# A matrix-memory cell's causal mask: from a product per decay tile to the unused rows of the decays' own operands

## The reference, cut to what matters

```
log_f_cum = concatenate([zeros, cumsum(log_sigmoid(fg), axis=2)], axis=2)
log_fg = where(ltr, (log_f_cum - log_f_cum^T)[:, :, 1:, 1:], -inf)
log_D = log_fg + ig^T
max_log_D = max(log_D, axis=-1)
D = exp(log_D - max_log_D)
C = (q @ k^T / sqrt(dh)) * D
Cn = C / (max(|C.sum(-1)|, exp(-max_log_D)) + EPS)
h = Cn @ v          # then normalised over dh and scaled
```

## Time and profile before

| | us |
|---|---|
| median of 3 runs | 823.45 (821.46 to 826.2) |
| the profiled execution, its own time | 822.99 |
| the profiled execution, span of the instructions | 821.2 |
| TensorE busy | 720.1 (88%) |
| VectorE busy | 503.7 (61%) |
| ScalarE busy | 418.2 (51%) |
| GpSimd busy | 387.2 (47%) |

### The profile page before, as it was taken

The page is one execution under the profiler, slowest core; times in us unless marked ns, Lnnn a source line. Parts: engine busy times, 40 slices in busy tenths (PEclk is TensorE's granted clock), DMA queues, the critical chain, the costliest instruction groups (busy, mean ns, idle before and its releaser), DMA issues.

```text
span 821.2 us, 20216 instructions
## 1 busy us (share of the span) xinstructions
PE 720.1 (88%) x7408; PEld 607.1 (74%) x7408; DVE 503.7 (61%) x992; ACT 418.2 (51%) x849; POOL 387.2 (47%) x587
## 2 busy tenths in 40 slices
PE   0874089999999998299999999999999999999993
PEld 0542057677767766178889999899999999999992
DVE  4772726667676766786525979443465767676740
ACT  0765336666666665443436323222456666666651
POOL 3111145778777776332211254214236575757553
PEclk9998559999999999599999999999999999999997
DMA  7882183545353530448772321332468888888854
GB/s 257 275 276 88 45 248 109 145 132 163 117 174 109 171 105 3 156 154 306 247 249 102 103 98 57 93 101 68 160 229 213 259 217 256 218 254 220 253 122 51
DMA packets 90720, 135.57 MB, mean 165 GB/s; under 512 B 16720, under 2 KB 44112, under 8 KB 90672
## 3 DMA queue, kind: packets, MB, share of 16 engines
q1 hardware_dynamic: 74128, 107.41, 39.8%
q0 software_dynamic: 7168, 17.04, 10.4%
q10 hardware_dynamic: 9376, 10.49, 3.9%
HBM read 92.32 MB, written 34.21 MB: 154 GB/s over the span
## 4 chain that ended last, share of the span: by engine, by line
PE 52%; DVE 3%; DMA 2%; POOL 1%; ACT 1%; issue 0%; SPq 0%; POOLq 0%; ACTq 0%
PE psH L1184 31%; PE psY L1201 15%; PE psT L1164 2%; PE psR L1225 2%; DMA xT<-over13l 1%; PE psT L1233 1%; DVE xnorm L1591 1%; DMA out<-ystage,sidx 1%; DVE xl L1414 1%; DVE stats L1482 1%; POOL out L1680 1%; PE psG L1240 1%; DVE over13h L1591 1%; ACT over13l L1362 0%; DVE over2l L1582 0%
## 5 line engine op out<-in xcount | busy, mean ns | idle before, releaser
L1184 PE MATMUL psH<-xh,w13h 128*128 128x256 f32 (+1 forms) x768 | 222.7, 290 | 3.0 <-DVE w13l L1426 3.0
L1184 PE MATMUL psH<-xh,w13l 128*128 128x256 f32 (+1 forms) x768 | 216.6, 282 | 0.0
L1184 PE MATMUL psH<-xl,w13h 128*128 128x256 f32 (+1 forms) x768 | 216.0, 281 | 0.0
L1648 POOL TENSOR_TENSOR hl<-sg,hh 128x256 fp32r<-128x256 f32 (+1 forms) x96 | 78.5, 823 | 212.8 <-ACT hh L1299 212.3
L1184 PEld LDWEIGHTS psH<-xh,w13h 128*128 128x128 f32 (+1 forms) x768 | 138.6, 180 | 12.2 <-issue 7.6
L1184 PEld LDWEIGHTS psH<-xl,w13h 128*128 128x128 f32 (+1 forms) x768 | 138.9, 181 | 0.7
L1184 PEld LDWEIGHTS psH<-xh,w13l 128*128 128x128 f32 (+1 forms) x768 | 138.8, 181 | 0.0
L1294 ACT ACTIVATE sg<-psH 128x256 f32<-128x256 f32 (+1 forms) x96 | 36.4, 379 | 132.4 <-PE psH L1184 131.5
L1420 DVE TENSOR_TENSOR sg<-sg,psH 128x256 f32<-128x256 f32 (+1 forms) x96 | 40.0, 417 | 99.7 <-ACT sg L1294 99.7
L709 ACT ACTIVATE dec<-ring 128x512 f32<-128x512 f32 x128 | 76.2, 595 | 44.9 <-PE ring L614 41.8
L785 DVE SCALAR_TENSOR_TENSOR dec<-psQ,dec 128x512 f32<-128x512 f32 x128 | 79.7, 682 | 11.9 <-PE psQ L626 10.1
(11 more groups left out here) (221 smaller groups left out, 1417.1 us busy)
## 6 DMA issues: line engine op xcount, KB each, us to landing
raw<-w13T SPq DMA_DIRECT2D x64, 352.0 KB, 4.3
gcT<-ctxT ACTq DMA_DIRECT2D x8, 1024.0 KB, 5.8
kT<-ctxT SPq DMA_DIRECT2D x16, 512.0 KB, 5.4
qst<-qT_all SPq DMA_DIRECT2D x16, 512.0 KB, 6.3
ctxs<-ctx SPq DMA_DIRECT2D x16, 512.0 KB, 3.5
xn<-xnorm SPq DMA_DIRECT2D x16, 512.0 KB, 3.7
out<-xres SPq DMA_DIRECT2D x16, 512.0 KB, 4.9
raw<-w2T SPq DMA_DIRECT2D x16, 512.0 KB
```

Source lines behind the costliest of these rows:

```text
L1184: last = nc.tensor.matmul(psH[m][0:n, v, :], w[wp][:, c, col:col + n], x[xp][:, c, :], start=(c == 0 and k == 0), stop=(c == DC - 1 and k ...
L1648: nc.gpsimd.tensor_tensor(hs[u.p][1][0:n, m, :], sg[0:n, m, :], hs[u.p][0][0:n, m, :].bitcast(F32), ALU.subtract).then_inc(hl_ready, 1)
```

## The change: the mask in the operands' other 122 rows, and a corner cleared on VectorE

The operands of the two rounds become tiles of their own with all 128 rows. Row 5+j of the stationary operand holds -1e30 at key j, and row 5+j of the moving one holds a one at every query before j, so each row masks one key; 122 rows mask the keys 1 to 121, and the last row all keys from 122 on for the queries before 122. The mask product goes. What the rows can't mask is the corner of the last 6 keys and 6 queries: a new operation of VectorE, `clear`, writes zeros above the diagonal there, in the weighed decays of all 16 heads at once, behind a tiny operation and a wait for `c_done`. TensorE's `values` waits for it (`cleared`). GpSimd makes the masked rows in the gate stage, and two new DMAs there copy them for the odd rounds. The copies of the queries for the first two batches are written straight to the buffers `qst` that the attention stage reads, so that two DMAs of 512 KB go; that makes room in SBUF.

```diff
+SPARE = P - 6
 # setup stage, GpSimd: identb and causal go
-            c.link(nc.gpsimd.tensor_copy(g.identb[:, :], g.ident[:, :]))
-            c.link(nc.gpsimd.memset(g.causal[:, :, :], 0.0))
-            c.link(nc.gpsimd.affine_select(out=g.causal[:, :, :], in_=g.causal[:, :, :], compare_op=ALU.is_ge,
-                                           fill=MASKED, base=0, pattern=[[0, 4], [1, P]], channel_multiplier=-1))
+            c.link(nc.gpsimd.memset(g.none[:, :], 0.0))
+            c.link(nc.gpsimd.memset(g.zeros[:, :], 0.0))
+            c.link(nc.gpsimd.memset(g.corner[:, :], 0.0))
+            c.link(nc.gpsimd.affine_select(out=g.corner[:, :], in_=g.corner[:, :], compare_op=ALU.is_ge,
+                                           fill=1.0, base=SPARE, pattern=[[1, P - SPARE]], channel_multiplier=-1))
...
 # norm_project_stage, ScalarE
-                    nc.scalar.activation(g.qT_all[:, bass.ds(n * DC, DC), :], psT[k][:, :, :],
-                                         ACT.Copy).then_inc(emptied, 1)
+                    to = g.qst[k][:, :, :] if r == 0 else g.qT_all[:, bass.ds((n - 2) * DC, DC), :]
+                    nc.scalar.activation(to, psT[k][:, :, :], ACT.Copy).then_inc(emptied, 1)
...
 # gate_stage, GpSimd and SyncE
-            nc.gpsimd.memset(g.aml[:, :, :], 1.0)
-            nc.gpsimd.memset(g.amr[:, :, :], 1.0)
+            for rows, outs, steps in ((maskl, g.aml, ((ALU.not_equal, MASKED, -5, 1, [[-1, P]], 0),
+                                                      (ALU.is_ge, MASKED, P - 2, -1, [[0, P - SPARE - 1]], SPARE + 1))),
+                                      (maskr, g.amr, ((ALU.is_gt, 1.0, 6, -1, [[1, P]], 0),))):
+                c.link(nc.gpsimd.memset(rows[:, :], 0.0))
+                for compare, fill, base, sign, pattern, lo in steps + ((ALU.is_ge, 1.0, -6, 1, [[0, P]], 0),):
+                    c.link(nc.gpsimd.affine_select(out=rows[:, lo:P], in_=rows[:, lo:P], compare_op=compare, fill=fill,
+                                                   base=base, pattern=pattern, channel_multiplier=sign))
+                nc.gpsimd.tensor_copy(outs[0][:, :, :], rows[:, :].rearrange("p (o t) -> p o t", o=1).broadcast_to(
+                    [P, NH, P])).then_inc(masks_ready, 1)
...
+            for k, rows in enumerate((g.aml, g.amr)):
+                sp.wait_ge(masks_ready, k + 1)
+                sp.dma_start(rows[1][:, :, :], rows[0][:, :, :]).then_inc(masks_kept, 16)
...
 # attention_stage, SyncE: load_keys
-                sp.dma_start(qst[u][:, :, :], g.qT_all[:, bass.ds(b * DC, DC), :]).then_inc(q_in[u], 16)
+                if b < 2:
+                    sp.sem_inc(q_in[u], 16)
+                else:
+                    sp.dma_start(qst[u][:, :, :], g.qT_all[:, bass.ds((b - 2) * DC, DC), :]).then_inc(q_in[u], 16)
...
 # attention_stage, TensorE: decay
-                    nc.tensor.matmul(out[:, gg * P:(gg + 1) * P], aml[32 * c:32 * c + 6, h, :], amr[32 * c:32 * c + 6, h, :],
-                                     start=(gg == 0), stop=(gg == 3), skip_group_check=True)
-                nc.tensor.matmul(out[:, :], g.identb[:, :], g.causal[:, :, :].rearrange("p a t -> p (a t)"), start=False,
-                                 stop=True, skip_group_check=True).then_inc(filled, 1)
+                    last = nc.tensor.matmul(out[:, gg * P:(gg + 1) * P], aml[c][:, h, :], amr[c][:, h, :], start=True, stop=True)
+                last.then_inc(filled, 1)
...
 # values
                 pe.wait_ge(v_ready, 2 * b + c + 1)
+                pe.wait_ge(cleared, 4 * i + r + 1)
...
 # attention_stage, VectorE
+            def clear(i, r):
+
+                c, lo = r % 2, P - 32
+                dve.wait_ge(c_done, 16 * i + 4 * r + 4)
+                nc.vector.tensor_tensor(g.none[:, 0:1], g.none[:, 1:2], g.none[:, 2:3], ALU.mult)
+                wide = lambda t: t[lo:P, :].rearrange("p (o t) -> p o t", o=1).broadcast_to([32, NH, P - SPARE])
+                nc.vector.copy_predicated(dec[c][lo:P, :, :, SPARE:P].rearrange("p k g t -> p (k g) t"),
+                                          wide(g.corner).bitcast(U32), wide(g.zeros)).then_inc(cleared, 1)
...
                     weigh(i, r, k, decay_use(i, r, k))
+                clear(i, r)
                 if r >= 1:
                     take(i, r - 1)
...
+            g.aml = [c.sb(f"aml{k}", [P, NH, P], BF16) for k in range(2)]
+            g.amr = [c.sb(f"amr{k}", [P, NH, P], BF16) for k in range(2)]
```

More of the change, by code:

```diff
@@ L383, in gate_stage @@
         parts = a.sb("gparts", [P, 2, 2, 3, S], BF16)
+        maskl, maskr = [a.sb("gmask" + n, [P, P], BF16) for n in "lr"]
+        pool_chain, masks_ready, masks_kept = map(a.sem, ("gt_pool", "gt_masks_ready", "gt_masks_kept"))
         psE = [a.ps(f"gpsE{k}", [P, 3, P]) for k in range(2)]
@@ L456, in _ @@
         def _(pool):
-            nc.gpsimd.memset(g.aml[:, :, :], 1.0)
-            nc.gpsimd.memset(g.amr[:, :, :], 1.0)
+            c = Chain(pool, pool_chain)
+            for rows, outs, steps in ((maskl, g.aml, ((ALU.not_equal, MASKED, -5, 1, [[-1, P]], 0),
[7 more added lines that the diff above has]
+                    [P, NH, P])).then_inc(masks_ready, 1)
             for q in range(2):
@@ L477, in _ @@
             sp.wait_ge(saved, 96)
+            sp.wait_ge(masks_kept, 32)
 def attention_stage(nc, g, d):
@@ L484, in attention_stage @@
         kT = [a.sb(f"kT{u}", [P, DC, S]) for u in range(2)]
-        qst = [a.sb(f"qst{u}", [P, DC, S]) for u in range(2)]
+        qst = g.qst
         ctxs = [a.sb(f"ctxs{u}", [P, 2, D]) for u in range(2)]
@@ L503, in attention_stage @@
         (filled, emptied, v_ready, qk_done, c_done, inter_done, back_done, sq_ready, o_taken, red_done, ve_ready,
-         x_done, t_ready, kk_ready, qsc_ready, state_zero, weights_set, y_ready, state_done, state_taken, chain, pch, ach) = map(
+         x_done, t_ready, kk_ready, qsc_ready, state_zero, weights_set, y_ready, state_done, state_taken, cleared, chain, pch, ach) = map(
             a.sem, ["at_" + n for n in (
@@ L507, in attention_stage @@
                 "red_done", "ve_ready", "x_done", "t_ready", "kk_ready", "qsc_ready", "state_zero", "weights_set", "y_ready", "state_done",
-                "state_taken", "chain",
+                "state_taken", "cleared", "chain",
                 "pool", "act")])
@@ L567, in load_decay @@
             def load_decay(b, c):
-                lo = 32 * c
-                sp.dma_start(aml[lo + 3:lo + 6, :, :], d.am[0][:, bass.ds(b, 1), :, c * P:(c + 1) * P].rearrange(
+                sp.dma_start(aml[c][3:6, :, :], d.am[0][:, bass.ds(b, 1), :, c * P:(c + 1) * P].rearrange(
                     "q b h t -> q (b h) t")).then_inc(am_in[c], 16)
-                sp.dma_start(amr[lo:lo + 3, :, :], d.am[1][:, bass.ds(b, 1), :, c * P:(c + 1) * P].rearrange(
+                sp.dma_start(amr[c][0:3, :, :], d.am[1][:, bass.ds(b, 1), :, c * P:(c + 1) * P].rearrange(
                     "q b h t -> q (b h) t")).then_inc(am_in[c], 16)
@@ L784, in weigh @@
                 dk = dec[c][:, k, :, :].rearrange("p a t -> p (a t)")
-                nc.vector.scalar_tensor_tensor(out=dk, in0=psQ[:, k, :], scalar=SCALE, in1=dk,
-                                               op0=ALU.mult, op1=ALU.mult).then_inc(c_done, 1)
+                weighed = nc.vector.scalar_tensor_tensor(out=dk, in0=psQ[:, k, :], scalar=SCALE, in1=dk, op0=ALU.mult, op1=ALU.mult)
+                weighed.then_inc(c_done, 1)
+            def clear(i, r):
[5 more added lines that the diff above has]
+                                          wide(g.corner).bitcast(U32), wide(g.zeros)).then_inc(cleared, 1)
             def take(i, r):
@@ L1768, in build @@
             c = Pools(nc, cell)
-            g.identb = c.sb("identb", [P, P], BF16)
-            g.causal = c.sb("causal", [P, 4, P], BF16)
             g.coef = c.sb("coef", [P, D])
-            g.qT_all = c.sb("qT_all", [P, B * DC, S])
+            g.qst = [c.sb(f"qst{u}", [P, DC, S]) for u in range(2)]
+            g.qT_all = c.sb("qT_all", [P, (B - 2) * DC, S])
             g.tmE = c.sb("tmE", [P, 3, B * NH])
-            g.aml = c.sb("aml", [38, NH, P], BF16)
-            g.amr = c.sb("amr", [38, NH, P], BF16)
+            g.aml = [c.sb(f"aml{k}", [P, NH, P], BF16) for k in range(2)]
+            g.amr = [c.sb(f"amr{k}", [P, NH, P], BF16) for k in range(2)]
+            g.corner = c.sb("corner", [P, P - SPARE])
+            g.zeros = c.sb("zeros", [P, P - SPARE])
+            g.none = c.sb("none", [P, 4])
             with ExitStack() as gates:
```

## The result

The changed kernel takes 803.9 us (median of 4, 802.19 to 804.49), the kernel before 824.4 beside it (median of 4); the ratio is 0.9751, with an interval of 0.9717 to 0.9785. That is 20 us less, and 804 was predicted. That the sum came out so exactly was luck: three of its terms were off, in different directions. The profiled execution has a span of 802.2 us against 821.2.

What follows compares the result with a forecast made beforehand. TensorE was taken to set the pace in the attention stage at the full clock. 14.8 batches x 1.12 gave 16.6 us, the start 2.5, together 19.1: 822.99 - 19.1 = 803.9, predicted as 804 us, range 797 to 815.

Steps and rivals of the forecast that it cites:

- A decay group without its mask: Attention stage, TensorE: four decay products of 128 rows take 0.33 us, against 0.64 for six rows with the mask.
- The round step by step: Attention stage, one batch on TensorE: odd round from 6.30 to 5.68 us, even round from 7.02 to 6.48, sum 12.16.
- Two chains of one length: Attention stage: the chain of `vals`, `normalise`, residual and `weigh` takes 12.17 us a batch, equal to TensorE's own path.
- Two chains disturb each other a little: Attention stage: the equal chains delay each other, so a batch was taken as 12.2 us, a gain of 1.12.
- `clear` costs nothing: VectorE, attention stage: some 0.5 us a round, covered by its wait for the squares; uncovered, 15 us in all.
- Rival 1: Attention stage: VectorE and GpSimd become the bound through `clear`; batch 12.6 to 13.0, time 810 to 816 us; chance 0.22.
- The start: Attention stage's beginning: DMA 1.2 and cheaper decay groups 2.9 put work 4.1 us ahead; 2.5 us won, bounds 1 and 7.
- The DMA's share: Start of the attention stage: the first queries no longer wait 1.31 us for the DMA of `qst`; 1.2 us taken.
- Rival 2: Attention stage: the clock rises earlier through full rows; each 3 us wins about 1.5; 796 to 801 us; chance 0.2.
- Rival 4: Attention stage: without dense 512-column products the clock falls back; 3.7 us lost a round, 841 us at 10 rounds; chance 0.05.
- The gate stage and the mixture stage: Gate stage: GpSimd's masked rows, some 2.6 us more, cost 0, at worst up to 3 us; mixture stage: 0.

Runs made afterwards that it cites:

- the third experiment: The run e3: the changed kernel with the 512-column mask product put back behind each four full-row decay products; 809.9 us, ratio 0.9842.
- e8: The changed kernel without the four small operations at the start of GpSimd's `normalise`; 798.2 us (one run).
- e7: The changed kernel with one of ScalarE's four state copies instead of four in every odd round; 803.9 us (one run).
- e9: The changed kernel with both cuts: one of four state copies, and `normalise` without its four small operations; 795.4 us (one run).
- e1: The changed kernel without VectorE's `clear` and TensorE's wait for it; 801.2 us, ratio 0.9735.
- e4: The kernel before with only the queries' buffers of the first two batches written directly, two DMAs of 512 KB fewer; 822.6 us, ratio 0.9986.
- e3: The changed kernel with the 512-column mask product put back behind each four full-row decay products; 809.9 us, ratio 0.9842.
- e2: The changed kernel with decay products of 6 rows only, no mask, and an exp scale of 0; 814.2 us.
- e6: The changed kernel with full-row products of ones where TensorE waits, around the starts of the attention and mixture stages; 801.7 us, ratio 0.9721.

## Why the prediction was right, and which of its steps were not

**A decay group without its mask, 0.33 us: right.** It takes 0.32. The reason given for the old price was only half of it. Going from the kernel before to the change by way of the third experiment, a batch falls by 0.42 when the six rows become all rows with the mask kept (`clear` added as well), and by 0.55 when the mask goes. By the other way, over six rows without a mask, it falls by 1.14 and rises by 0.17. The prediction's 0.64 less 0.33 covers both effects without telling them apart.

**The round step by step: the even one nearly right, the odd one 0.25 short.** The forecast was 5.68 + 6.48 = 12.16, and the trace has 5.92 + 6.39 = 12.31 in the batch shown. The state products start 2.19 after the even queries (2.17 forecast), behind ScalarE's exp. In the odd round the gather was put at 1.43; it starts at 1.80 in the batch shown and at 1.55 in the next, since it waits for `take`, as line 671 says (`o_taken`). `take` was forecast to come 0.15 late and declared harmless, because its residual waits for GpSimd anyway. The gather, the other one that waits for it, was left out. In the next batch (199.18 to 211.53) it is the other chain that is late: the load of the even queries waits for the last `weigh`.

```profile
200.73 0.35 PEld L675 LDWEIGHTS psO<-vals,kkw 128*32 128x32 f32 x32 [0.22 <-DVE sm L830]
...
205.13 0.98 PEld L644 LDWEIGHTS psQ<-qst,kT 32*128 32x128 f32 x32 [0.30 <-DVE dec L804]
```

The batches take turns, an odd round of 5.92 behind the late gather and one of 5.95 behind the late `weigh`. With `normalise` shortened (e8) the gather starts at 1.55 to 1.64 and the queries don't wait: the odd rounds are 5.76 and the batch 12.16, the forecast's own sum. So the term that was mis-sized is what the two chains cost each other: 0.04 a batch was taken (12.2 for 12.16), and it is 0.17. The 0.13 too little make 1.8 us in 14 batches. The sum of 12.16 is itself partly luck, since its odd round is 0.08 too short and its even one 0.08 too long.

**Two chains of one length: right**, and the best supported step (e7, e8, e9). "Two chains disturb each other a little" was right in kind; the 12.2 made of it is 12.33. The sign named for it, the even queries starting right behind the last `weigh`, shows in every second batch.

**`clear` costs nothing: nearly.** 0.12 us a batch (e1); its size in the profile was forecast at 0.5 us a round and is 1.0, since it gets long beside GpSimd's scaled queries. Rival 1 had this as its mechanism and 12.6 to 13.0 as its price, 0.4 to 0.8 over the forecast; that was three to seven times too dear.

**The start: mis-sized.** Forecast 3.4 with the part of a batch, measured 7.9 in this profile, 6.3 in the second one (28.88 less 22.54). The DMA's share was right, 1.3 to 1.5 for 1.2. The rest was reckoned with a clock that rises when it did. It is the full rows that bring it up: with the mask kept the stretch goes from 27.39 (six rows, direct queries) to 22.03 (all rows), with the mask gone from 26.68 to 21.03. So some 5.5 us of the 7.9 are due to the full rows, or 4.1 of 6.3 with the changed kernel's second profile. How much of that is the clock alone no run separates; an estimate from the changed kernel's two profiles, where a clock 5.7 us earlier goes with a start 1.5 us shorter, gives 3.3 for the 12.6 us between e4 and e3 and 4.6 for the 17.5 between e2 and the changed kernel. The mask's going shows as 0.7 and 1.0 us, which is within the 1.5 that the same kernel varies by. Rival 2 had the right mechanism; its price, 1.5 us for each 3 us, is about twice what those two profiles show.

**Rival 4, the clock that falls back**, did not happen, but it does where the rows stay six: with the mask products taken away (e2) the clock fell six times (814.2 us). With full rows it stayed up until TensorE's work in the stage was done, unless products of ones had brought it up early (e6). Without them 10 us of the gain would be gone, the late start included.

**The gate stage and the mixture stage: right**, both within 0.4 us. GpSimd's two masked copies took 1.89 us each and ended 0.5 us ahead of VectorE's run, which started 7.5 us into the stage, as before (7.6).

**The 2.0 us lost ahead of the gate stage** can't be told from chance. The norm stage's copies have the same size, and 77.06 and 79.06 both lie inside the spread of 76.3 to 79.1. So 804 was met by three errors that cancel: the start gave 4.5 us more than forecast, the batches 2.1 less, and 2.0 were lost ahead of the gate stage.

## What to carry to other kernels

When a product is removed, list who waits for each thing that comes late, not only the next in the queue: here the residual behind `take` was followed, and a product of TensorE on another line paid. Two chains of one length hide each other's gain; cut both before saying that neither matters. And a small operation that is put in an engine's waiting time may double in the profile and cost next to nothing, so that neither its busy time nor the engine's share says what it costs; leave it out once and look.

## What the runs showed of the hardware

- At like busy time TensorE's granted clock differed with the rows of the decay products. With decay products of all 128 rows it came up 6.7 to 13.5 us after the stage's start (the kernels with products of ones apart), with six rows 19.3 to 25.3. At six rows it stayed at 0.50 (1.2 GHz) while TensorE was busy for 7.74 of 8.00 us, and fell from 1.00 behind a stretch with 84% busy; at all rows it held 1.00 with 86%. Two starts of the same kernel, the clock up at 7.8 and at 13.5 us, differed by 1.5 us.
- A product whose shape in rows and columns differs from the one ahead stands about 0.1 us later than one of the same shape: the mask's load 0.33 behind the first load of six rows, 0.19 behind that of all rows.
- A predicated copy of 32 x 96 on VectorE took 0.30 us at the median and 1.35 beside a GpSimd operation of 1.27 us on 128 x 512 elements in SBUF; the operation of one element took from 0.16 to 1.18, and the one of 1.04 ended with such a GpSimd operation.
